# Adding x1 to the experts' sum by identity products on TensorE, with ScalarE copying it out

## What is computed

```python
x = x + s6(layernorm(x))                    # selective state space block
x = x + moe(layernorm(x))                   # 8 experts, 2 chosen, and a shared one

# s6: 256 hidden channels, 16 states, rank 64, 4 taps
uo = x @ W_in.T;  u, o = split(uo)
u = silu(conv4(u) + conv_b)
g = u @ W_gate.T;  delta_lo, b, c = split(g)
delta = softplus(delta_lo @ W_delta.T + delta_bias)
h = exp(A * delta_t) * h + (delta_t * u_t) * b_t      # for each token t
y_t = sum_over_states(h * c_t) + D * u_t
out = (y * sigmoid(o) * o) @ W_out.T

# moe: top 2 of softmax(x @ gate_w.T), weights normalised, times 2.5
out = sum_e combine_e * (silu(x @ w_gate_e) * (x @ w_up_e)) @ w_down_e
      + (silu(x @ sw_gate) * (x @ sw_up)) @ sw_down
```

## Time and profile before

| | |
|---|---|
| median of 3 runs | 1240.33 us (1239.35 to 1240.44) |
| the profiled execution | 1238.7 us, span of its trace 1237.0 us |
| TensorE products | busy 1123.3 us (91% of the span), 9075 instructions |
| TensorE weight loads | busy 919.1 us (74%) |
| VectorE | busy 1066.9 us (86%) |
| GpSimd | busy 1067.5 us (86%) |
| ScalarE | busy 1011.0 us (82%) |
| mean granted TensorE clock | 0.966 of full speed; full from 150 us to 1100 us |

### The profile page before, as it was taken

The page is one execution under the profiler, slowest core; times in us unless marked ns, Lnnn a source line. Parts: engine busy times, 40 slices in busy tenths (PEclk is TensorE's granted clock), DMA queues, the critical chain, the costliest instruction groups (busy, mean ns, idle before and its releaser), DMA issues. The chain is left out here.

```text
span 1237.0 us, 25691 instructions
## 1 busy us (share of the span) xinstructions
PE 1123.3 (91%) x9075; PEld 919.1 (74%) x9075; DVE 1066.9 (86%) x1700; ACT 1011.0 (82%) x2119; POOL 1067.5 (86%) x502
## 2 busy tenths in 40 slices
PE   3456999999999999999999999999999999998887
PEld 2334778878778787887787878877878788876676
DVE  3277899999999999999998999999999999999854
ACT  2778888888888888888988888889888988897642
POOL 3299899999999999999998999999999999999810
PEclk8767999999999999999999999999999999999899
DMA  4444433344434333444343334443433344434000
GB/s 119 109 111 105 102 84 85 107 109 109 99 92 112 87 82 101 109 109 113 79 113 86 82 101 109 108 112 80 113 94 83 93 109 110 107 79 103 5 6 9
DMA packets 71482, 115.05 MB, mean 93 GB/s; under 512 B 8174, under 2 KB 30395, under 8 KB 71355
## 3 DMA queue, kind: packets, MB, share of 16 engines
q1 hardware_dynamic: 67178, 110.71, 35.0%
q10 hardware_dynamic: 4176, 2.70, 0.8%
HBM read 41.04 MB, written 5.24 MB: 37 GB/s over the span
## 5 line engine op out<-in xcount | busy, mean ns | idle before, releaser
L410 POOL TENSOR_TENSOR inject<-rep,bc 128x1024 f32<-128x1024 f32 x256 | 604.6, 2384 | 20.2 <-DMA rep<-dd 20.2
L420 POOL TENSOR_TENSOR read<-state,bc 128x1024 f32<-128x1024 f32 x192 | 452.2, 2376 | 10.2 <-DVE state L687 8.8
L687 DVE TENSOR_TENSOR_SCAN state<-decay_ps,inject 128x1024 f32<-128x1024 f32 x192 | 432.0, 2279 | 13.8 <-ACT decay_ps L489 13.0
L489 ACT ACTIVATE decay_ps<-rep,neg_a 128x255 f32<-128x255 f32 x1024 | 427.0, 465 | 8.9 <-DVE state L687 3.5
L936 PE MATMUL acc_ps<-ffn_down,features 128*128 128x128 f32 (+1 forms) x1792 | 244.8, 281 | 0.5 <-DVE features L716 0.5
L936 PEld LDWEIGHTS acc_ps<-ffn_down,features 128*128 128x128 f32 (+1 forms) x1792 | 220.3, 192 | 23.4 <-DVE features L716 7.4
L902 PE MATMUL work_ps<-xn2T_part,ffn_gate 128*128 128x256 f32 x1344 | 219.4, 300 | 6.7 <-ACT g_silu L476 3.0
L476 ACT ACTIVATE g_silu<-work_ps 128x512 f32<-128x512 f32 x224 | 134.9, 602 | 105.4 <-PE work_ps L902 94.8
L902 PEld LDWEIGHTS work_ps<-xn2T_part,ffn_gate 128*128 128x128 f32 x1344 | 180.0, 193 | 52.1 <-ACT g_silu L476 22.7
L911 PE MATMUL work_ps<-xn2T_part,ffn_up 128*128 128x256 f32 x1344 | 193.2, 284 | 0.0
L708 DVE TENSOR_TENSOR features<-g_silu,work_ps 128x512 f32<-128x512 f32 x224 | 149.8, 682 | 47.8 <-PE work_ps L911 47.4
(11 more groups left out here) (130 smaller groups left out, 1250.5 us busy)
## 6 DMA issues: line engine op xcount, KB each, us to landing
rep<-dd SPq DMA_DIRECT2D x256, 256.0 KB, 4.7
bc<-bc_rows SPq DMA_DIRECT2D x64, 512.0 KB, 4.6
x_in<-in_L_attn_x_dram SPq DMA_DIRECT2D x32, 128.0 KB, 2.1
out_dram<-result SPq DMA_DIRECT2D x32, 128.0 KB, 1.8
bc_rows<-g_sb SPq DMA_DIRECT2D x32, 32.0 KB
state<-in_L_ffn_w_gate_dram ACTq DMA_DIRECT2D x1, 704.0 KB, 4.4
read<-in_L_ffn_w_up_dram ACTq DMA_DIRECT2D x1, 704.0 KB, 5.9
ffn_down<-in_L_ffn_w_down_dram ACTq DMA_DIRECT2D x1, 704.0 KB, 7.2
```

The costliest lines, as they stand in the source:

```text
L410: pool.tensor_tensor(inject[:, at % RI], du_all, b_all, ALU.mult).then_inc(inject_done, 1)
L420: pool.tensor_tensor(read[:, at % RR], state[:, at % RS], c_all, ALU.mult).then_inc(read_done, 1)
L489: last = act.activation(decay_ps[:, at % 2, j, 1:T], rep[(HALVES * n + half) % RP][:, j, 0, 1:T], ACT.Exp, scale=neg_a[:, col:col + 1])
L687: dve.tensor_tensor_scan(to, decays, inject[:, at % RI].rearrange("p j t -> p (j t)"), 0.0, ALU.mult, ALU.add).then_inc(state_done, 1)
```

## The change

Four things:

1. `down(0)` now issues, for each half j of the tokens, a product of the identity with `x1[:, j, :]` into `down_ps` ahead of the chunk's own product. `down_ps` then holds x1 plus the experts' sum. The start flag moves to the first of them.
2. The addition L768 on VectorE is gone. ScalarE copies `down_ps` to `result`, between the cast of `xnT_part` (L528) and the decays of group 3.
3. Orders on ScalarE: `combT` is copied behind the second cast of `xnT_part`; Ln and the negated mean go ahead of the decays of group 5; z is copied ahead of xn2, and both ahead of the decays of group 6; the casts of `xn2T_part` stand one ahead and one behind the decays of group 7. The casts of the expert weights, which occur once in body -1, move to the front of it.
4. Orders on VectorE and TensorE, shown below. GpSimd's and SyncE's orders stay as they are.

```diff
 # ScalarE
+                if on(-3):
+                    n = k - 3
+                    act.wait_ge(down_mm, CHUNKS * (n + 1))
+                    act.wait_ge(stored[n % 2], 16 * (n // 2))
+                    act.wait_ge(y_taken, HALVES * min(k, SEQS))
+                    act.copy(result[n % 2][:].rearrange("p j d -> p (j d)"), down_ps).then_inc(result_done, 1)
                 if on(0):
                     decays(k, 3)
...
-                if on(-2):
-                    act.wait_ge(combT_mm, f + 1)
-                    act.wait_ge(cb_mm, COMBS * f)
-                    act.copy(combT[:], combT_ps).then_inc(combT_done, 1)
                 if on(2):
                     n = k + 2
                     act.wait_ge(xnT_rest, n + 1)
                     act.copy(xnT_parts[1][:, TAPS - 1:], xnT_ps).then_inc(xnT_low, 1)
+                if on(-2):
+                    act.wait_ge(combT_mm, f + 1)
+                    act.wait_ge(cb_mm, COMBS * f)
+                    act.copy(combT[:], combT_ps).then_inc(combT_done, 1)
...
 # VectorE
-                if on(-3):
-                    n = k - 3
-                    dve.wait_ge(down_mm, CHUNKS * (n + 1))
-                    dve.wait_ge(stored[n % 2], 16 * (n // 2))
-                    dve.tensor_tensor(result[n % 2][:].rearrange("p j d -> p (j d)"), down_ps,
-                                      x1[n % 2][:].rearrange("p j d -> p (j d)"), ALU.add).then_inc(result_done, 1)
...
 # TensorE, down(chunk, n)
                     for j in range(TILES):
+                        if chunk == 0:
+
+                            pe.matmul(down_ps[:, j * DIM:(j + 1) * DIM], ident[:], x1[n % 2][:, j, :],
+                                      start=fresh and j == 0, stop=False, skip_group_check=True)
                         last = pe.matmul(down_ps[:, j * DIM:(j + 1) * DIM], features[0:r, chunk, j * P:(j + 1) * P],
-                                         ffn_down[0:r, chunk, :], start=fresh and j == 0, stop=(chunk == CHUNKS - 1),
+                                         ffn_down[0:r, chunk, :], start=False, stop=(chunk == CHUNKS - 1),
                                          skip_group_check=True)
```

More of the change, by code:

```diff
@@ L1121, in body @@
                 if on(-2):
[L1122 to L1123 removed]
+                    down(7, f)
+                    down(8, f)
+                    down(9, f)
                 if on(0):
```

134 lines of the change are left out of this document (66 added, 68 removed).

## The result

The changed kernel takes 1254.51 us as the median of four runs (1250.24 to 1254.63), the kernel before 1239.84 (1239.18 to 1240.44, four runs on the same chip). The quotient of these medians is 1.0118; the ratio on record is 1.0099, 95% interval 1.0071 to 1.0126. Both say slower, the medians by 14.7 us. The profiled execution is the fastest of the four, 1250.24, and 11.5 us over that of before (1238.7). The other three are 4.3 us longer; their mean granted clock is 0.963 to 0.965 of full speed, that of the profiled one 0.969.

What follows compares the result with a forecast made beforehand. It took a ring of ScalarE (silu(3) to silu(4)) and TensorE (gates(5) to gates(3)) as the bound. 30 bodies x 0.6 = 18, plus 0.9 for draining: 19 us, profiled 1257.7, median 1259; forecast 1253 to 1265, whole range 1242 to 1270.

Steps and rivals of the forecast that it cites:

- the ring: Loop setting the body's pace: ScalarE from silu(3) to silu(4), then TensorE from gates(5) to the next gates(3); body 35.04 us.
- S: ScalarE's leg from silu(3) to silu(4), 11.91 us before; the result's copy was to lengthen it by 0.17.
- VectorE's walk: VectorE chain from dd through scan(4) and pair(4): 1.4 us idle, silu(6) +0.3, then scan(5) +0.65 with Ln's move.
- the slack for gates(2): Time pair(0) on VectorE had to spare before delaying gates(2) on TensorE, put at 0 to 0.3 us.
- The cast `xn2T_part`: ScalarE's cast, one set of decays fewer ahead of it: starts at 505.1, ready at 505.5.
- rival C: Faster: VectorE's chain to `comb_parts` decides, 0.41 us less there saves 0.33 to 0.41 a body, 1229 us; chance 10%.
- they stand on the leg of TensorE in the ring, so nothing covers them: Four identity instructions in front of and inside down(0) on TensorE cost their full 0.45 us a body.
- TensorE's wait of 0.25 for the cast: New wait at TensorE's `neg_identr` product for ScalarE's `xn2T_part`, 0.1 to 0.3 us, delaying gates(0).
- The merged spreads: On TensorE, two blocks of two `csel` products become one block of four: -0.24 us a body.
- the 0.1 for one block of down products fewer: On TensorE, five blocks of down products become four, saving some 0.1 us for an uncovered weight load.
- -0.05 for the read waits: TensorE, coming later, no longer waits for GpSimd's `read`: -0.05 us a body on average.
- the drain: The two draining bodies at the end also carry the identity products, adding 0.9 us.

Runs made afterwards that it cites:

- e3: Kernel before, all orders kept, but ScalarE copies the result, L768 is gone and x1 is left out: 1246.82 us, ratio 1.0045.
- e1: Kernel before with the two transposes of xn issued twice, between gates(3) and gates(5) on TensorE: 1243.49 us, ratio 1.0007.
- e4: Changed kernel without the two identity products, x1 left out of the result: 1253.58 us, ratio 1.0095.
- e6: Changed kernel with scan(4) ahead of dd again on VectorE and without the identity products, x1 left out: 1246.39 us, ratio 1.0051.
- e7: Kernel before with all its orders, but x1 added by identity products in down(0) and the result copied by ScalarE: 1248.42 us, ratio 1.0068.
- e2: Kernel before with the two transposes of xn2 issued twice, between gates(5) and gates(3) on TensorE: 1244.34 us, ratio 1.0022.
- e8: Kernel before with spread_comb(5) directly behind spread_comb(4) on TensorE, two blocks made one: 1242.41 us, ratio 1.0013.
- e5: Changed kernel with scan(4) ahead of dd again on VectorE, as before: 1248.21 us, ratio 1.0072.
- e9: e6 with down(4) moved ahead of TensorE's neg_identr product for xn2: 1247.93 us, ratio 1.0051.
- e10: Kernel before with both spreads together and sum_states(6) and down(10) moved behind ups(0): 1251.47 us, ratio 1.0090.

## Why the prediction was right, and where it was off

**Right: slower, and by about this.** 1254.51 lies in the range, 4.5 us under the value; the body was put at 35.5 to 35.7 and is 35.60. Part of this is luck. The sum was made for the profiled execution, 1257.7, and that took 1250.24, below the 1253 to 1265 of the forecast; the median is inside because the other three executions are 4.3 us longer.

**Right: the ring, and S.** That silu(3) to silu(4) is a serial leg, that the copy costs 0.26 - 0.09 = 0.17 there, and that work between gates(3) and gates(5) on TensorE is free: e3 and e1 show each of them, to 0.02.

**Right: VectorE's walk, with a size off.** It said 1.4 us of idle time ahead of dd (1.40), silu(6) released by the features and 0.3 later (0.17 in the table and 0.17 of S: 0.34), scan(5) 0.65 later (0.38 + 0.17 = 0.55). The 0.1 too much is Ln with the negated mean, taken at 0.4, of which 0.21 arrives, less the 0.04 by which silu(6) is later still. Of the slack for gates(2), put at 0 to 0.3, there is next to none: before it started 0.13 behind the end of pair(0), where with a wait it is 0.08, and the 0.38 of scan(5) reach gates(3) whole. The cast `xn2T_part` was put at 505.1; 10.90 behind a silu(4) at 494.16 is 505.06.

**Right: rival C kept small.** Taking 0.41 us a body from VectorE, at 93% busy, showed no gain beside the copy (e3). The Trainium skill, page Perfetto Trace Analysis, section Identifying the Most-Contended Engine, has the engine with the highest occupancy optimized first. By the shares of the earlier trace rows that is GpSimd with 94%, with VectorE at 93% just behind it, so the rule points to GpSimd first and not, as the prediction had it, to VectorE. The waits decided it, not the shares.

**Wrong: "they stand on the leg of TensorE in the ring, so nothing covers them".** The size, 0.45, is as measured; the cover was misjudged. In the new orders all of it is covered (e4, e6), in the old ones half (e7, e2). The reasoning had one body whose only wait, 0.22 for GpSimd's `read`, seemed to make that leg solid. But e2's 0.45 moved gates(0) by only 0.23, and in e8 0.19 saved bring gates(0) no earlier; and beside TensorE's path runs VectorE's, which ends at the same moment. A leg without visible waits is not a leg alone.

**Wrong, small: TensorE's wait of 0.25 for the cast.** The prediction had TensorE at that product at 505.2 to 505.4 and took 0.25 of its range of 0.1 to 0.3. It starts at 494.16 + 11.32 = 505.48 and finds the cast just done, with no wait. Only without the identity is there one (e4). gates(0) is 0.24 + 0.17 = 0.41 later, not 0.5. But that is with no wait in it, where the other terms alone gave 0.22: they were put too low. The merged spreads give 0.19 (e8), not 0.24, and the 0.1 for one block of down products fewer stands on no row, and no run separates it.

**Mis-sized: -0.05 for the read waits, and the drain.** These terms made the total too high. The old kernel's mean body is 0.15 over its median, the new one's 0.05. So the mean grows by 0.45 (35.20 to 35.65) where the commonest grows by 0.55, and 0.6 was taken. I had counted a body 0.21 longer as one among many and had not averaged over all. About 0.07 of that 0.10 is the one body of 1.86 us too much, in which the clock fell; the new orders have no such body, and the prediction had no term for it. It is not the longer body that absorbs it: e7 is as long as e5 and keeps its 0.15. In the trace the sum is then 26 x 0.45 = 11.7, with 2.2 ahead of the first result and 3.6 less behind, where 0.9 more was forecast for the drain. What shortens the drain was not looked into.

Two errors met: the identity's 0.45 went where VectorE's path ended last anyway, and since the total took the later of both paths, its size hardly moved the sum. The 0.6 was right to 0.05 for the commonest body by the VectorE path, and 0.15 too high for the mean.

The Trainium skill, page TensorE: Matmul & The Clock Gate, section Back-to-back issue gap, has some 81 ns for a weight load with a product of 128 columns. The trace disagrees for these `f32` ones: 0.22 to 0.23 for two, at full clock. By either price the body would be the same here, as e4 shows.

## What to carry to other kernels

Where several engines are over 85% busy, write the body as a sum of legs between two recurring instructions and, for each leg, every chain that ends at its last instruction, with the time each has to spare; an added piece costs only what exceeds that, and orders laid out to make room for it can lengthen the chain that was tied with it. Price an order by the latest input of each step that moves up: dd ahead of a scan made VectorE idle for 1.4 us on an input that was not ready yet. And compare the mean body with the commonest one before counting delays one for one: look at the longest bodies by themselves, at what TensorE waited for in them and at the clock behind that wait. A wait of 0.4 us there stood ahead of a body 1.86 us too long.

Read a wait against a kernel in which its releaser is long done. If the idle time is the same there, it is not a wait.

## What the runs showed of the hardware that was not expected

- The same four instructions cost 0, 0.16 or 0.20 us a body by place (e1, e7, e2) although TensorE is busy 97% of the stretch: 919.96 of 950 us.
- Where gates(2) waits for pair(0) on VectorE (changed kernel, e4, e9), it starts 0.08 us behind its end, and the next block follows 0.79 behind gates(2) instead of 0.71 to 0.74.
- The weight loads are idle for 0.41 us ahead of gates(3), behind a sum of states of eight products, in every kernel, whether VectorE was done shortly before or long before (changed kernel and e10).
- In a stretch that is at full clock by its mean, the granted clock can fall to half for some us behind a wait of TensorE: 0.40 us of waiting for `read` at 650.82 in the kernel before, then 0.50 of full speed from 652 to 654 and full again from 655. It happened in eleven bodies of six kernels, each with such a wait of 0.2 to 1.5 us, and in none of the other seven.
- A copy of 128x256 from PSUM on ScalarE takes 0.36 us by its own row and 0.26 from start to start; only the second is what the next instruction feels. Of an Ln and a small activation with 0.30 from start to the next decay, 0.21 reach the scan behind.
